# Summing the eight product blocks of each chunk with one strided reduction on VectorE, four transposes of the sums in place of sixteen, and the gate's projection ahead of them

## The chip, the cores and the metric

The kernel runs on one core of one Trainium2 chip. A core has a matrix engine (PE, TensorE), a vector engine (DVE, VectorE), an activation engine (ACT, ScalarE), a general engine (POOL, GpSimd) and a queue engine (SP, SyncE) that here only issues transfers. Each engine works through its own list of instructions in order; semaphores tie the lists together. The metric is device time in microseconds (us), from the median of several runs. Lower is better.

## The reference, cut to what matters

All values are 32-bit floats. `x` and the context are (16, 256, 512): 16 positions, 256 rows, 512 channels-in-time. The 256 rows make 32 heads of 8 rows. The layer is two blocks, each added to its input through a tanh gate:

```python
# block 1, per head h: eight rows i, eight rows j, a causal convolution over l (512)
kv  = einsum('bhil,bhjl->bijhl', ctx, ctx)
y   = causal_conv(kv, ssm_kernel[h]) + kv * D[h]
o[b, j, h, l] = sum over i of  y[b, i, j, h, l] * layernorm(x)[b, h, i, l]
x   = x + tanh(g_xattn) * o
# block 2, per row of 16 positions: a gated mixture-of-two linear attention
z   = layernorm(x);  s = silu(z_prev * w0 + z * w1)
q, k, v, g = silu(s @ Wq), s @ Wk, s @ Wv, s @ Wg
out = (silu(g) * layernorm(attention(q, k, v))) @ Wout
x   = x + tanh(g_ffn) * out
```

The sum over `i` is over eight products. It is this sum that the change makes in another way.

## The kernel before

One pass of the main loop handles one head. On chip, a head's 512 time steps are four chunks of 128 (`CH` = 4), the time step within a chunk lies on the 128 partitions, and the free dimension holds the 8 rows times 16 positions (`ROW` = 128 columns). `kv` is symmetric in i and j, so it is computed by rotations: four rotations of 128 columns and half a rotation, 576 columns a chunk.

The loop is software-pipelined and fully unrolled. `run` calls `step` for h = -2 to 32; a step does the tail of head h-1 (attention output, output projection), the back of head h (projections, scores), the front of head h+1 (convolution, products, sums) and the preparation of head h+2 (products of the context, layer norm). Every engine has its own `step`, written out by hand, so the order of work on an engine is the order of the code, with waits on semaphores between. 31 steps (h = 0 to 30) hold a back and a front.

The part around the change, for one head:

- PE runs the convolution of chunk `lc` into a PSUM bank (`conv`, L282).
- DVE multiplies the bank with the normalised `x` (`multiply`, L733, and for the half rotation `multiply_last`, L770). For each chunk this leaves eight blocks of 128 columns in `z_terms[:, lc, :]`, one for each of the eight rotations or mirrored rotations, which are the eight terms of the sum over i.
- DVE adds the last four blocks onto the first four (`add_halves`, L751, instruction at L756): once for chunks 0 and 1 together (1024 columns out), once each for chunks 2 and 3 (512 columns out). Semaphore `sum_done`.
- PE transposes the remaining four blocks of each chunk and lets PSUM add them up: 16 transposes of 128 x 128 into bank 2 (`add_transposed`, L271, instruction at L277). Semaphore `xo_ps`.
- DVE reads bank 2 and makes the new `x` (`x2`, L889), its statistics (L892 to L900); POOL takes the inverse root (L649), ACT the normalised `z` (L614), with which PE begins the next step (transposes at L268).

What stands behind the transposes of the sums on PE in a step: the gate's projection (`project` into bank 5, 12 matmuls, L426), the transposes of the expanded queries and keys (L428 and L431, which wait for `expand` on DVE, L763 to L768, and for `gatedT_low`, L877, the last reader of bank 7), the output projection of the head before (L440, 12 matmuls), and `scores` (L341), 16 matmuls, which waits among others for `x2_ready` since bank 2 is one of the four score banks. DVE then waits for the output projection (`out_sb`, L913) and masks the scores (L760). ACT copies `gatedT_high` (L588), the two last parts of the context products (`kv_round`, L487), the gate (`gate_sb`, L597), `qeT` and `keT` (L603, L606).

Of the kernel before, what the change touches and what calls it, by code (L numbers as in the profile page):

```python
# [7 lines left out]
ALU = mybir.AluOpType  # L8
ACT = mybir.ActivationFunctionType
F32 = mybir.dt.float32  # L10
F32R = mybir.dt.float32r
AX_X = mybir.AxisListType.X

P = 128
# [15 lines left out]
def flamingo_gated_layer(nc, x, ctx_t, g_xattn, g_ffn, ssm_kernel, ssm_D, conv_w, Wq, Wk, Wv, Wg,  # L30
# [35 lines left out]
    with ExitStack() as stack:  # L66
# [8 lines left out]
        def setup_sb(name, *free):  # L75
            return setup.enter_context(nc.sbuf_tensor(name, [P, *free], F32))
# [51 lines left out]

        setup = ExitStack()
        w_all = setup_sb("w_all", CH, PROJ)  # L130
        w_out = setup_sb("w_out", CH, L)
        w_tmp = z_terms[:, :, 0:DV]
        router = setup_sb("router", RH * HDV, RATIO)
        router_d = setup_sb("router_d", RH * HDV)
        taps = setup_sb("taps", P + L)
        taps_p = setup.enter_context(nc.sbuf_tensor("taps_p", [P, 2, P + L], F32R))
        setup.close()

        y_raw = sb("y_raw", CH, P)
        qk_sb = sb("qk_sb", 2 * RH, HDK)  # L140
        rot_a = sb("rot_a", 2 * RH, HDK)
# [10 lines left out]
        out_sb = sb("out_sb", 2, L)  # L152
        yT_p = parts("yT", CH, P)
        gatedT_p = parts("gatedT", CH, P)
# [110 lines left out]
        def _(eng):  # L265
# [4 lines left out]

            def add_transposed(h1):  # L271


                for c in range(CH):
                    eng.wait_ge(sum_done[max(c, 1)], h1 + 1)
                    for i in range(NROT):
                        ins = nc.tensor.matmul(bank[2][:, c * P:(c + 1) * P], z_terms[:, c, i * ROW:(i + 1) * ROW], ident,  # L277
                                               is_transpose=True, start=(c == 0 and i == 0), stop=(i == NROT - 1),
                                               skip_group_check=True)
                ins.then_inc(xo_ps, 1)  # L280
# [45 lines left out]
            def step(t, p, q, tail, back, front, pre):  # L326
# [85 lines left out]
                if tail:  # L412
# [5 lines left out]
                    transpose4(bank[7], lambda c: gated[:, c * P:(c + 1) * P], gatedT_ps)  # L418
                if front:
                    if pre:  # L420
                        eng.wait_ge(qx_ready, h + 3)
                    add_transposed(h + 1)
                if back:
                    if can_wait(h):
                        eng.wait_ge(mask_done[2], h)
                    project(bank[5], yT_p, w_all_p, G0, DV, g_ps, y_low, h + 1)  # L426
                    eng.wait_ge(qke_ready, h + 1)
                    transpose4(bank[3], lambda c: qke[:, 4 * c:4 * c + 4, :], qeT_ps)  # L428
                    if tail:
                        eng.wait_ge(gatedT_ready, h)  # L430
                    transpose4(bank[7], lambda c: qke[:, RH + 4 * c:RH + 4 * c + 4, :], keT_ps)  # L431
# [15 lines left out]
        def _(eng):  # L447
# [41 lines left out]
            def step(t, p, q, tail, back, front, pre):  # L489
# [94 lines left out]
                if tail:  # L584
                    eng.wait_ge(gatedT_ps, h)
                    if can_wait(h - 1):
                        eng.wait_ge(out_ps, h - 1)
                    eng.activation(gatedT_p[0][:, :, :], bank[7][:, :].rearrange("p (c n) -> p c n", c=CH), ACT.Copy  # L588
                                   ).then_inc(gatedT_high, 1)
                if pre:  # L590
                    kv_round(p, 2, h + 2)
                    kv_round(p, 3, h + 2)
                if back:
                    eng.wait_ge(g_ps, h + 1)
                    if can_wait(h):
                        eng.wait_ge(gated_ready, h)
                    eng.activation(gate_sb[:, :], bank[5][:, :], ACT.Silu).then_inc(gate_ready, 1)  # L597
                if back:
                    eng.wait_ge(qeT_ps, h + 1)
                    if can_wait(h):  # L600
                        for r in range(CH):
# [4 lines left out]
                    eng.activation(keT[:, :, :], bank[7][:, :].rearrange("p (c n) -> p c n", c=CH), ACT.Copy  # L606
                                   ).then_inc(keT_sb, 1)
                if front:
                    eng.wait_ge(rstd2_ready, h + 2)
# [78 lines left out]
        def _(eng):  # L688
# [44 lines left out]
            def multiply(p, lc, h1):  # L733
# [3 lines left out]
                if lc == 0:  # L737
                    eng.wait_ge(qx_ready, h1 + 1)
                    if can_wait(h1):
                        eng.wait_ge(xo_ps, h1)  # L740
                q = qx[:, 1 - p, lc, 0:1]
# [8 lines left out]

            def add_halves(chunks, h1):  # L751

                eng.wait_ge(mul_last, h1 + 1)
                eng.wait_ge(mul_done[chunks.stop - 1], h1 + 1)
                half = NROT * ROW
                eng.tensor_tensor(z_terms[:, chunks, 0:half], z_terms[:, chunks, 0:half], z_terms[:, chunks, half:2 * half],  # L756
                                  ALU.add).then_inc(sum_done[chunks.stop - 1], 1)

# [26 lines left out]
            def step(t, p, q, tail, back, front, pre):  # L785
# [64 lines left out]
                if front:  # L850
                    add_halves(slice(0, 2), h + 1)
                if tail:
# [12 lines left out]
                if front:  # L865
                    multiply(p, 3, h + 1)
                    add_halves(slice(2, 3), h + 1)
                    add_halves(slice(3, 4), h + 1)
                if back:
# [4 lines left out]
                if tail:  # L874
# [3 lines left out]
                                      gatedT_p[0][:, :, :].bitcast(F32), ALU.subtract).then_inc(gatedT_ready, 1)  # L878
                if back:
                    eng.wait_ge(rot_ready, h + 1)  # L880
                    if can_wait(h):
                        eng.wait_ge(keT_ps, h)
                        eng.wait_ge(qeT_ps, h)
                    expand()
                if front:
# [84 lines left out]
```

## Time and profile before

| | us |
|---|---|
| median of 3 runs (lowest, highest) | 923.17 (922.25, 925.02) |
| profiled execution, whole | 923.74 |
| profiled execution, span from first to last instruction | 921.9 |
| PE busy | 856.9 (93% of the span) |
| POOL busy | 730.2 (79%) |
| DVE busy | 720.5 (78%) |
| ACT busy | 435.7 (47%) |

Times in the profile are of one execution. An engine's timeline row gives the start, the time until the last of its instructions ended, the engine, the line, the operation and, in brackets, how long the engine sat idle before it and what ended the wait. Neighbouring instructions of an engine overlap by some tens of nanoseconds, so what an instruction costs its engine is read from one start to the next.

### The profile page before, as it was taken

To read this page: it belongs to the slowest core of one execution; us is meant where nothing else is said; L and a number is where in the kernel's file an instruction comes from. 1 tells how busy PE (TensorE), PEld (TensorE's weight loads), DVE (VectorE), ACT (ScalarE), POOL (GpSimd) and SP (SyncE) were. 2 spreads that over 40 slices of the span, in tenths; PEclk is the share of its full clock that TensorE was granted. 3 is DMA by queue.
4 is the path that set the end of the run, shared out by engine and by line. 5 is a ranking of instruction groups with operands and counts; after the bars stand their busy time and mean duration, and the time that the engine had idled before them with its cause. 6 is when DMAs were issued, how large, how long until landed. Compare 5 with 4: busy or idle time off the path is not lost.

```text
span 921.9 us, 17871 instructions
## 1 busy us (share of the span) xinstructions
PE 856.9 (93%) x6528; PEld 724.3 (79%) x6528; DVE 720.5 (78%) x1528; ACT 435.7 (47%) x938; POOL 730.2 (79%) x613
## 2 busy tenths in 40 slices
PE   0578999999999999999999999999999999999973
PEld 0467888888888888888888888888888888888852
DVE  4867787987778889877787897778878877788742
ACT  2454544545545444554544545545445455454330
POOL 6568898788889888888899888888988888887331
PEclk9889999999999999999999999999999999999996
DMA  8211211222221122222211222222112222210000
GB/s 284 60 53 52 59 26 44 64 63 65 64 64 43 25 61 64 64 64 65 62 34 35 61 64 64 65 63 61 26 42 64 64 64 63 64 46 12 2 12 23
DMA packets 25990, 52.44 MB, mean 57 GB/s; under 512 B 2544, under 2 KB 3696, under 8 KB 25904
## 3 DMA queue, kind: packets, MB, share of 16 engines
q1 hardware_dynamic: 22304, 46.59, 18.7%
q10 hardware_dynamic: 3600, 4.72, 1.6%
q8 instruction: 52, 0.85, 0.4%
q14 instruction: 34, 0.28, 0.1%
HBM read 42.75 MB, written 8.55 MB: 56 GB/s over the span
## 4 chain that ended last, share of the span: by engine, by line
PE 86%; DVE 5%; issue 4%; DMA 1%; ACT 1%; POOL 1%; POOLq 0%; ACTq 0%; DVEq 0%
PE bank L319 37%; PE bank L290 23%; PE bank L268 9%; PE bank L277 6%; PE bank L352 4%; PE bank L337 4%; PE bank L303 2%; DMA w_all<-in_L_ffn_Wv 1%; PE bank L306 1%; DVE z_terms L756 1%; DVE w_all L719 0%; PE bank L402 0%; DVE z_terms L743 0%; DVE w_all_low L725 0%; POOLq L66 0%
## 5 line engine op out<-in xcount | busy, mean ns | idle before, releaser
L290 PE MATMUL bank<-kv_pair,toep 128*128 128x512 f32 x960 | 247.9, 405 | 11.4 <-DVE z_terms L747 6.6
L643 POOL TENSOR_TENSOR kv_pair<-kv,kv_pair 128x576 fp32r<-128x576 f32 x128 | 182.3, 1436 | 54.9 <-ACT kv_pair L487 54.9
L290 PEld LDWEIGHTS bank<-kv_pair,toep 128*128 128x128 f32 x960 | 177.2, 192 | 53.1 <-DVE z_terms L747 12.6
L634 POOL TENSOR_TENSOR kv<-kx 128x512 f32<-128x512 f32 x128 | 174.4, 1363 | 6.7 <-DMA const<-shape_consts 6.7
L649 POOL TENSOR_TENSOR o_rstd<-o_ve,minus_half 128x16 f32<-128x16 f32 x32 | 93.1, 2909 | 82.6 <-DVE o_ve L815 82.6
L487 ACT ACTIVATE kv_pair<-kv 128x576 fp32r<-128x576 f32 x128 | 87.9, 688 | 108.2 <-POOL kv L637 108.2
L319 PE MATMUL bank<-w_all_high,yT_high 128*128 128x512 f32 (+2 forms) x512 | 120.2, 356 | 2.8 <-DVE gated L856 2.8
L756 DVE TENSOR_TENSOR z_terms<-z_terms 128x512 f32<-128x512 f32 (+1 forms) x96 | 117.4, 1249 | 0.0
L319 PE MATMUL bank<-w_all_low,yT_high 128*128 128x512 f32 (+2 forms) x512 | 111.8, 340 | 0.0
L319 PE MATMUL bank<-w_all_high,yT_low 128*128 128x512 f32 (+2 forms) x512 | 106.1, 339 | 0.0
L913 DVE TENSOR_TENSOR out_sb<-bank,x 128x512 f32<-128x512 f32 x32 | 22.1, 691 | 105.6 <-PE bank L319 105.6
L760 DVE TENSOR_TENSOR att<-bank,const 128x512 f32<-128x512 f32 x128 | 79.5, 683 | 16.7 <-PE bank L352 16.7
L319 PEld LDWEIGHTS bank<-w_all_low,yT_high 128*128 128x128 f32 x512 | 83.7, 189 | 11.2
L319 PEld LDWEIGHTS bank<-w_all_high,yT_low 128*128 128x128 f32 x512 | 81.2, 188 | 11.5
L743 DVE TENSOR_TENSOR z_terms<-bank,qx 128x512 f32<-128x512 f32 x128 | 85.4, 667 | 4.3 <-PE bank L290 4.3
L319 PEld LDWEIGHTS bank<-w_all_high,yT_high 128*128 128x128 f32 x512 | 78.9, 190 | 8.9 <-DVE gated L856 3.2
L637 POOL TENSOR_TENSOR kv<-kx 128x64 f32<-128x64 f32 x128 | 73.5, 574 | 0.0
L747 DVE TENSOR_TENSOR z_terms<-bank,qx 128x384 f32<-128x384 f32 x128 | 69.9, 546 | 0.0
L667 POOL TENSOR_TENSOR rot_a<-qk_sb,const 128x512 f32<-128x512 f32 x32 | 66.2, 2069 | 2.5 <-ACT qk_sb L557 2.5
L277 PE MATMUL bank<-const,z_terms 128*128 128x128 f32 x512 | 62.5, 274 | 5.4 <-DVE z_terms L756 5.4
L503 ACT ACTIVATE y_raw<-bank,w_conv 128x128 f32<-128x128 f32 x128 | 36.6, 369 | 61.9 <-PE bank L268 61.9
L649 POOL TENSOR_TENSOR rstd<-ve,minus_half 128x1 f32<-128x1 f32 x64 | 41.2, 643 | 28.3 <-DVE ve L900 22.2
(102 smaller groups left out, 1588.7 us busy)
## 6 DMA issues: line engine op xcount, KB each, us to landing
toep<-taps_dram SPq DMA_DIRECT2D x32, 512.0 KB, 7.1
kx<-in_ctx SPq DMA_DIRECT2D x32, 384.0 KB, 7.4
x_in<-in_x SPq DMA_DIRECT2D x32, 256.0 KB
out_x<-out_sb SPq DMA_DIRECT2D x32, 256.0 KB
w_all<-in_L_ffn_Wv ACTq DMA_DIRECT2D x1, 1024.0 KB, 11.9
w_all<-in_L_ffn_Wg ACTq DMA_DIRECT2D x1, 1024.0 KB, 9.9
w_out<-in_L_ffn_Wout ACTq DMA_DIRECT2D x1, 1024.0 KB, 16.2
router<-in_L_ffn_router_w ACTq DMA_DIRECT2D x1, 512.0 KB, 7.3
```

Of the source, the lines that this page charges most:

```text
L268: ins = nc.tensor.transpose(dst[:, c * P:(c + 1) * P], src(c), ident)
L277: ins = nc.tensor.matmul(bank[2][:, c * P:(c + 1) * P], z_terms[:, c, i * ROW:(i + 1) * ROW], ident, is_transpose=True, start=(c == 0 and ...
L290: ins = nc.tensor.matmul(bank[lc % 2][:, :], toep[:, 1 - p, a, (lc - mc) * P:(lc - mc + 1) * P], kv_p[b][:, 1 - p, mc, 0:FULL], start=(mc ...
L319: ins = nc.tensor.matmul(dst[:, 0:cols], src_p[a][:, c, :], w_p[b][:, c, c0:c0 + cols], start=(i == 0 and c == 0), stop=(i == len(PASSES) ...
L487: eng.activation(kv_p[0][:, p, c, :], kv[:, c % 2, :], ACT.Copy).then_inc(kv_high[c], 1)
L634: eng.tensor_tensor(view(kv[:, c % 2, 0:FULL], [[ROW, NROT], [1, ROW]]), view(kx[:, p, c, 0:ROW], [[0, NROT], [1, ROW]]), view(kx[:, p, c, ...
L637: eng.tensor_tensor(kv[:, c % 2, FULL:FULL + HALF], kx[:, p, c, 0:HALF], kx[:, p, c, HALF:2 * HALF], ALU.mult).then_inc(kv_made[c], 1)
L643: eng.tensor_tensor(kv_p[1][:, p, c, :], kv[:, c % 2, :], kv_p[0][:, p, c, :].bitcast(F32), ALU.subtract).then_inc(kv_ready[c], 1)
L649: eng.tensor_tensor(dst[:, 0:n], src[:, 0:n], minus_half[:, 0:n], ALU.pow).then_inc(done, 1)
L743: eng.tensor_tensor(view(z_terms[:, lc, 0:1], [[ROW, NROT], [1, ROW]]), view(y[:, 0:1], [[ROW, NROT], [1, ROW]]), view(q, [[NB, NROT], [1, ...
L756: eng.tensor_tensor(z_terms[:, chunks, 0:half], z_terms[:, chunks, 0:half], z_terms[:, chunks, half:2 * half], ALU.add).then_inc(sum_done[ ...
L760: eng.tensor_tensor(att[:, r, :, :], bank[SCORE_BANKS[r]][:, :].rearrange("p (c n) -> p c n", c=CH), view(mask[:, 0:1], [[0, CH], [1, P]]) ...
```

## The change

- `add_halves` goes. In its place `sum_terms` issues one `tensor_reduce` a chunk, four a head: 128 outputs, each the sum of eight inputs. The view puts the rotation innermost with a step of `ROW` = 128 floats (512 bytes), so each instruction reads 1024 floats of `z_terms`, and no two that follow each other are neighbours in memory. The result goes into `z_sum`, which is the buffer `y_raw` under another name.
- `add_transposed` with its 16 transposes becomes `transpose_sums` with 4, on `z_sum`.
- On PE the gate's projection moves ahead of the transposes of the sums.
- On ACT the gate's copy moves ahead of `kv_round` 2, and `kv_round` 3 moves behind the copy of `keT`.
- On DVE `expand` moves ahead of `ratio` and `gatedT_low`.
- The wait on `xo_ps` moves from `multiply` of chunk 0 (which now waits on the last `sum_done` of the head before) into `sum_terms`. Two setup buffers and `yT` change their place in SBUF.

```diff
-            def add_transposed(h1):
+            def transpose_sums(h1):
                 for c in range(CH):
-                    eng.wait_ge(sum_done[max(c, 1)], h1 + 1)
-                    for i in range(NROT):
-                        ins = nc.tensor.matmul(bank[2][:, c * P:(c + 1) * P], z_terms[:, c, i * ROW:(i + 1) * ROW], ident,
-                                               is_transpose=True, start=(c == 0 and i == 0), stop=(i == NROT - 1),
-                                               skip_group_check=True)
+                    eng.wait_ge(sum_done[c], h1 + 1)
+                    ins = nc.tensor.transpose(bank[2][:, c * P:(c + 1) * P], z_sum[:, c, :], ident)
                 ins.then_inc(xo_ps, 1)
...
+                if back:
+                    if can_wait(h):
+                        eng.wait_ge(mask_done[2], h)
+                    project(bank[5], yT_p, w_all_p, G0, DV, g_ps, y_low, h + 1)
                 if front:
                     if pre:
                         eng.wait_ge(qx_ready, h + 3)
-                    add_transposed(h + 1)
-                if back:
-                    if can_wait(h):
-                        eng.wait_ge(mask_done[2], h)
-                    project(bank[5], yT_p, w_all_p, G0, DV, g_ps, y_low, h + 1)
+                    transpose_sums(h + 1)
...
-            def add_halves(chunks, h1):
+            def sum_terms(c, h1):
                 eng.wait_ge(mul_last, h1 + 1)
-                eng.wait_ge(mul_done[chunks.stop - 1], h1 + 1)
-                half = NROT * ROW
-                eng.tensor_tensor(z_terms[:, chunks, 0:half], z_terms[:, chunks, 0:half], z_terms[:, chunks, half:2 * half],
-                                  ALU.add).then_inc(sum_done[chunks.stop - 1], 1)
+                eng.wait_ge(mul_done[c], h1 + 1)
+                if can_wait(h1):
+                    eng.wait_ge(xo_ps, h1)
+                eng.tensor_reduce(z_sum[:, c, :], view(z_terms[:, c, 0:1], [[1, ROW], [ROW, 2 * NROT]]), AX_X, ALU.add
+                                  ).then_inc(sum_done[c], 1)
...
-                    add_halves(slice(0, 2), h + 1)
+                    sum_terms(0, h + 1)
+                    sum_terms(1, h + 1)
...
-                    add_halves(slice(2, 3), h + 1)
-                    add_halves(slice(3, 4), h + 1)
+                    sum_terms(2, h + 1)
+                    sum_terms(3, h + 1)
+                if back:
+                    eng.wait_ge(rot_ready, h + 1)
+                    if can_wait(h):
+                        eng.wait_ge(keT_ps, h)
+                        eng.wait_ge(qeT_ps, h)
+                    expand()
```

PE, from the transposes of `gated` to the output projection, in the kernel before (`qke` holds expanded queries and keys, bank 5 is the gate's):

```order
L268 MATMUL bank7<-const,gated 128x128 x4
L277 MATMUL bank2<-const,z_terms 128x128 x16
L319 MATMUL bank5<-w_all_high,yT_high 128x512 x4
L319 MATMUL bank5<-w_all_low,yT_high 128x512 x4
L319 MATMUL bank5<-w_all_high,yT_low 128x512 x4
L268 MATMUL bank3<-const,qke 128x128 x4
```

The same stretch of PE in the changed kernel, where `y_raw` is the buffer that holds the sums:

```order
L269 MATMUL bank7<-const,gated 128x128 x4
L317 MATMUL bank5<-w_all_high,yT_high 128x512 x4
L317 MATMUL bank5<-w_all_low,yT_high 128x512 x4
L317 MATMUL bank5<-w_all_high,yT_low 128x512 x4
L277 MATMUL bank2<-const,y_raw 128x128 x4
L269 MATMUL bank3<-const,qke 128x128 x4
```

The 12 matmuls of the gate stand ahead of the sums, and the transposes of the sums are 4; the transposes of `qke` follow them directly.

DVE, from the selection masks to the new `x`, in the kernel before:

```order
L842 TENSOR_SCALAR u<-bank6 128x16
L756 TENSOR_TENSOR z_terms<-z_terms 128x2x512
L856 TENSOR_TENSOR gated<-bank4,o_rstd 128x512
L861 TENSOR_TENSOR gated<-gated,gate_sb 128x512
L864 RECIPROCAL rth1<-th1 128x16
L743 TENSOR_TENSOR z_terms<-bank1,qx 128x512
L747 TENSOR_TENSOR z_terms<-bank1,qx 128x3x128
L756 TENSOR_TENSOR z_terms<-z_terms 128x512 x2
L873 TENSOR_TENSOR ratio<-rth1,bank6 128x16
L877 TENSOR_TENSOR gatedT_low<-bank7,gatedT_high 128x512
L765 TENSOR_TENSOR qke<-rot_a,sel 128x1024
L889 SCALAR_TENSOR_TENSOR x2<-bank2,gates,x_in 128x512
```

The same stretch of DVE in the changed kernel:

```order
L843 TENSOR_SCALAR u<-bank6 128x16
L757 TENSOR_REDUCE y_raw<-z_terms 128x128 x2
L858 TENSOR_TENSOR gated<-bank4,o_rstd 128x512
L863 TENSOR_TENSOR gated<-gated,gate_sb 128x512
L866 RECIPROCAL rth1<-th1 128x16
L743 TENSOR_TENSOR z_terms<-bank1,qx 128x512
L747 TENSOR_TENSOR z_terms<-bank1,qx 128x3x128
L757 TENSOR_REDUCE y_raw<-z_terms 128x128 x2
L766 TENSOR_TENSOR qke<-rot_a,sel 128x1024
L881 TENSOR_TENSOR ratio<-rth1,bank6 128x16
L885 TENSOR_TENSOR gatedT_low<-bank7,gatedT_high 128x512
L891 SCALAR_TENSOR_TENSOR x2<-bank2,gates,x_in 128x512
```

Two reductions stand where one add of two chunks stood, ahead of the `gated` pair; two where two adds of one chunk stood; and `expand` (`qke`) is ahead of `ratio` and `gatedT_low`.

## Rows read from the trace of the kernel before

**Rows 1.** The page, part 1: busy time and share of the span.

```profile
PE 856.9 (93%) x6528; PEld 724.3 (79%) x6528; DVE 720.5 (78%) x1528; ACT 435.7 (47%) x938; POOL 730.2 (79%) x613
```

**Rows 2.** The page, part 4: the chain that ended last, by engine.

```profile
PE 86%; DVE 5%; issue 4%; DMA 1%; ACT 1%; POOL 1%; POOLq 0%; ACTq 0%; DVEq 0%
```

**Rows 3.** The view of waits: who waited for whom, total us, times, longest.

```profile
DVE out_sb L913 <- PE bank L319: 105.6, 32, 4.4
...
DVE yT_low L807 <- ACT y_raw L528: 25.9, 32, 2.3
```

**Rows 4.** The chain in order of time, one step: start, us, what.

```profile
416.21 0.44 PE bank L268 x4
416.65 1.75 PE bank L277 x16
418.40 2.78 PE bank L319 x12
...
422.05 2.75 PE bank L319 x12
```

**Rows 5.** Timeline of PE, same step: start, length, operation.

```profile
421.02 1.03 PE L268 MATMUL bank<-const,qke 128*128 128x128 f32 x8
...
424.73 1.17 PE L352 MATMUL bank<-qeT,keT 32*128 32x128 f32 x32
```

**Rows 6.** Timeline of DVE, the same step.

```profile
399.47 2.48 DVE L760 TENSOR_TENSOR att<-bank,const 128x512 f32<-128x512 f32 x4 [0.39 <-PE bank L352]
...
411.05 1.22 DVE L756 TENSOR_TENSOR z_terms<-z_terms 128x1024 f32<-128x1024 f32 x1
412.18 0.69 DVE L856 TENSOR_TENSOR gated<-bank,o_rstd 128x512 f32<-128x512 f32 x1
...
415.06 2.43 DVE L756 TENSOR_TENSOR z_terms<-z_terms 128x512 f32<-128x512 f32 x2
417.41 0.16 DVE L873 TENSOR_TENSOR ratio<-rth,bank 128x16 f32<-128x16 f32 x1
...
418.09 1.56 DVE L765 TENSOR_TENSOR qke<-rot_a,sel 128x1024 f32<-128x1024 f32 x1
419.58 0.74 DVE L889 SCALAR_TENSOR_TENSOR x<-bank,gates,x_in 128x512 f32<-128x512 f32 x1
...
424.84 0.69 DVE L913 TENSOR_TENSOR out_sb<-bank,x 128x512 f32<-128x512 f32 x1 [3.25 <-PE bank L319]
425.93 2.48 DVE L760 TENSOR_TENSOR att<-bank,const 128x512 f32<-128x512 f32 x4 [0.39 <-PE bank L352]
```

**Rows 7.** Groups by form on DVE: count, busy us, mean ns, idle before.

```profile
L756 DVE TENSOR_TENSOR z_terms<-z_terms 128x512 f32<-128x512 f32 x64 | 76.0, 1226 | 0.0
...
L812 DVE TENSOR_REDUCE o_var<-o_sq 128x16 f32<-128x512 f32 x32 | 22.0, 687 | 7.3 <-ACT o_sq L533 4.4
...
L702 DVE TENSOR_TENSOR router_d<-router 128x512 f32<-128x512 f32 x1 | 1.7, 1700 | 0.7 <-DMA w_all<-in_L_ffn_Wv 0.7
```

**Rows 8.** Single lines, L756 and L765: shortest, median, longest duration in ns.

```profile
L756 DVE TENSOR_TENSOR z_terms<-z_terms x96: 673/1216/2219, 41.7 to 866.2; 128x512 f32<-128x512 f32 x64, 128x1024 f32<-128x1024 f32 x32
...
L765 DVE TENSOR_TENSOR qke<-rot_a,sel x32: 1215/1559/1842, 73.3 to 891.9; 128x1024 f32<-128x1024 f32 x32
```

**Rows 9.** Timeline of POOL: beside L702 at 14.67 us, and beside step 399.47.

```profile
14.61 1.21 POOL L634 TENSOR_TENSOR kv<-kx 128x512 f32<-128x512 f32 x1
15.78 0.77 POOL L637 TENSOR_TENSOR kv<-kx 128x64 f32<-128x64 f32 x1
...
421.59 0.55 POOL L649 TENSOR_TENSOR rstd<-ve,minus_half 128x1 f32<-128x1 f32 x1 [0.28 <-DVE ve L900]
```

**Rows 10.** Timeline of ACT, the same step.

```profile
423.76 0.81 ACT L614 ACTIVATE z<-x,nmr,rstd 128x512 f32<-128x512 f32 x1
```

**Rows 11.** Timeline of DVE, step h = -1.

```profile
41.72 1.34 DVE L756 TENSOR_TENSOR z_terms<-z_terms 128x1024 f32<-128x1024 f32 x1
...
46.08 0.75 DVE L889 SCALAR_TENSOR_TENSOR x<-bank,gates,x_in 128x512 f32<-128x512 f32 x1 [0.75 <-PE bank L277]
```

More of the change, by code:

```diff
@@ L129, in flamingo_gated_layer @@
         setup = ExitStack()
+        taps = setup_sb("taps", P + L)
+        taps_p = setup.enter_context(nc.sbuf_tensor("taps_p", [P, 2, P + L], F32R))
         w_all = setup_sb("w_all", CH, PROJ)
@@ L134, in flamingo_gated_layer @@
         router_d = setup_sb("router_d", RH * HDV)
-        taps = setup_sb("taps", P + L)
-        taps_p = setup.enter_context(nc.sbuf_tensor("taps_p", [P, 2, P + L], F32R))
         setup.close()
         y_raw = sb("y_raw", CH, P)
+        z_sum = y_raw
+        yT_p = parts("yT", CH, P)
         qk_sb = sb("qk_sb", 2 * RH, HDK)
@@ L152, in flamingo_gated_layer @@
         out_sb = sb("out_sb", 2, L)
-        yT_p = parts("yT", CH, P)
         gatedT_p = parts("gatedT", CH, P)
@@ L418, in step @@
                     transpose4(bank[7], lambda c: gated[:, c * P:(c + 1) * P], gatedT_ps)
-                if front:
-                    if pre:
-                        eng.wait_ge(qx_ready, h + 3)
-                    add_transposed(h + 1)
                 if back:
@@ L426, in step @@
                     project(bank[5], yT_p, w_all_p, G0, DV, g_ps, y_low, h + 1)
+                if front:
+                    if pre:
+                        eng.wait_ge(qx_ready, h + 3)
+                    transpose_sums(h + 1)
+                if back:
                     eng.wait_ge(qke_ready, h + 1)
@@ L589, in step @@
                                    ).then_inc(gatedT_high, 1)
-                if pre:
-                    kv_round(p, 2, h + 2)
-                    kv_round(p, 3, h + 2)
                 if back:
@@ L597, in step @@
                     eng.activation(gate_sb[:, :], bank[5][:, :], ACT.Silu).then_inc(gate_ready, 1)
+                if pre:
+                    kv_round(p, 2, h + 2)
                 if back:
@@ L607, in step @@
                                    ).then_inc(keT_sb, 1)
+                if pre:
+                    kv_round(p, 3, h + 2)
                 if front:
@@ L739, in multiply @@
                     if can_wait(h1):
-                        eng.wait_ge(xo_ps, h1)
+                        eng.wait_ge(sum_done[CH - 1], h1)
                 q = qx[:, 1 - p, lc, 0:1]
@@ L878, in step @@
                                       gatedT_p[0][:, :, :].bitcast(F32), ALU.subtract).then_inc(gatedT_ready, 1)
-                if back:
-                    eng.wait_ge(rot_ready, h + 1)
-                    if can_wait(h):
-                        eng.wait_ge(keT_ps, h)
-                        eng.wait_ge(qeT_ps, h)
-                    expand()
                 if front:
```

## The prediction

> **What bounds the kernel now.** I read the busy shares first: PE is at 93%, DVE at 78%, POOL at 79% [rows 1]. Then the chain that ended last: 86% of it is PE [rows 2]. So PE sets the pace, and the waits agree: the largest wait of DVE is for PE's output projection, 105.6 us in 32 times, 3.3 us a step [rows 3]. That wait is the slack that DVE has in a step. Last I read one step as a timeline of DVE and as the chain of PE. Masks begin at 399.47 and again at 425.93, so a step takes 26.46 us [rows 6], and there are 31 such steps. I count time in a step from 399.47, so that the masks stand at t = 0.
>
> **The change on PE.** The 16 transposes of the sums take 1.75 us of the chain, 0.109 each; four others take 0.44 [rows 4]. Twelve go, so PE saves 1.31 us a step and its own work falls to 26.46 - 1.31 = 25.15 us. If nothing else were late, that would be 31 x 1.31 = 41 us, or 883 us. The gate's projection is 2.78 us [rows 4], the same before and after; standing first, it gives the sums that much more time.
>
> **The change on DVE.** Before, the sums cost DVE 412.18 - 411.05 = 1.13 us for chunks 0 and 1, and 417.41 - 415.06 = 2.35 us for chunks 2 and 3, in all 3.48 us a step [rows 6]. The second pair is dear because POOL reads at the same time: an add of 512 columns takes 1.226 us on average [rows 7], but the shortest of the line takes 0.673 [rows 8].
>
> After, there are four reductions of 1024 inputs. Nothing in the trace reads single floats 512 bytes apart, so I bound one reduction, R, from both sides. The low end: a reduction of 512 neighbouring inputs takes 0.687 us [rows 7], and the add of 1024 columns takes 1.22 [rows 6], 0.55 more than the shortest add of 512; with that slope R = 0.69 + 0.53 = 1.22 us. No row on DVE goes below this rate for 32-bit data, so I exclude a lower one. The high end: one instruction reads single floats, every second one, for both of its operands: L702, 512 columns in 1.700 us [rows 7]. Taken whole, less 0.16 us of fixed cost (0.69 less 0.53), that is 3.0 ns a column and R = 3.24 us.
>
> L702 is the row nearest in kind, but POOL worked beside it, and POOL's second instruction there took 0.77 us [rows 9], so part of the 1.700 is contention. An add of the same size under contention takes 1.226 on average [rows 7]. I put the rest, 0.474 us or 0.93 ns a column, down to the step. It was paid with two stepped operands, the reduction has one. Between half of it (0.46) and all of it (0.93) I take the middle, 0.69 ns a column, so R = 1.22 + 1024 x 0.69 ns = 1.93 us. The ends are kept for the range. What speaks against this: the first POOL instruction beside L702 ended at 15.82, and L702 ended at 16.37, which is 0.55 us later, as long as 512 columns take at the full rate. If DVE merely stood behind POOL, stepping by 8 bytes cost nothing. It remains that 512 bytes is another step than 8.
>
> The Trainium skill has a measured rule on this ("Vector Engine (DVE) Microarchitecture Reference", section Measured stream behaviour on trn2): a port keeps its full rate only while consecutive elements come as at least two neighbouring words, and a source that hops at every element cost 1.73 ns a column where a contiguous one cost 1.05. By that page R would be about 1.92 us, an estimate. It also names an exception, a one-source operation hopping between two regions and writing one word per two reads, which ran at the full rate; by that R would be 1.22. No row here shows either.
>
> **What a step takes after.** An instruction of 1.22 us costs DVE 1.13, as the next one starts 0.09 earlier [rows 6]; so a reduction costs s = R - 0.09. Along DVE and then PE:
>
> - from the masks to the first sum, unchanged: 411.05 - 399.47 = 11.58;
> - two sums: 2s; then the `gated` pair, the reciprocal and the products of chunk 3, unchanged: 415.06 - 412.18 = 2.88; two sums: 2s;
> - `expand`: 418.09 to 419.58 is 1.49 beside POOL, but its shortest is 1.215 [rows 8], so 1.15 if POOL has finished its products by then, which it has when DVE is late; `ratio` and `gatedT_low`: 418.09 - 417.41 = 0.68;
> - about 0.1 for the semaphore, then PE: the second four transposes of `qke`, which write bank 7 after `gatedT_low` has read it, 0.44; the output projection 2.75 [rows 4]; and from its end at 424.80 to the next masks at 425.93, 1.13, in which PE runs the scores [rows 5]. (The transposes of `qke` themselves are the eight of 421.02 [rows 5].)
>
> That is 11.58 + 2.88 + 1.15 + 0.68 + 0.1 + 0.44 + 2.75 + 1.13 + 4s = 20.71 + 4s. With R = 1.93, s = 1.84 and the step is 28.07 us, 1.61 more than before. PE, with 25.15 us of work, waits about 2.9 us a step: some 0.3 for `gated` (it moves back by 2s - 1.13 = 2.55 us, and had about 2.2 of room), some 1.5 in front of the sums, the rest for `expand` and `gatedT_low`. What hides behind what: the new `x` starts at t = 23.65 instead of 20.11. From it to the end of `z` is 5.0 us before [rows 6, 10], but 1.2 of that is ACT still busy when POOL's root was ready at 422.14 [rows 9]; the true chain is about 3.8, so `z` is there at 27.5, before PE wants it at about 28.0. The `scores` wait for `x` is met too, as 24.4 is before 27. ACT's moves cost nothing: ACT is busy 47% [rows 1], and the copies that PE waits for come first. POOL's last parts of the context products wait behind the root and land some 2 us later against the step; POOL's work of 730.2 us is 23 us a step and fits in 28.
>
> In step h = -1 PE is idle and the sums lie on the chain: from 41.72 to the new `x` at 46.08 [rows 11]. Four sums for three adds: 4 x 1.84 - 2.54 = +4.8, and the last transposes take some 0.4 less: +4.4 us.
>
> The sum: 923.7 + 31 x 1.61 + 4.4 = 978 us. The profiled execution (923.74, its span 921.9) is 0.6 above the median of 923.17, so this is 978 for the median too.
>
> **The rivals.**
>
> 1. *The strided read runs at the full rate: faster.* R = 1.22, s = 1.13. The chain gives 20.71 + 4.52 = 25.23, and with `expand` still beside POOL 25.57, against PE's 25.15. So 0.89 to 1.3 us a step are won: 923.7 - 31 x 0.89 + 1.6 = 898, at best 885. For it: 0.55 us after POOL in L702 [rows 7, 9], the reduction of one source at the full rate, and that it stands out of POOL's way. Against it: the inputs have no neighbours at all. The two cases part at 4s = 26.46 - 20.71, so R = 1.53 us: below it the kernel is faster, above it slower. This is also the result of the skill's exception.
> 2. *The step costs what both operands of L702 paid, or more.* R = 2.17 gives s = 2.08 and a step of 29.03: 923.7 + 31 x 2.57 + 5.4 = 1009 us. At R = 3.24 the step is 33.3 and the time about 1146. For it: L702 as it stands. Against it: the contention in it.
> 3. *R lands beside the break-even of 1.53* and the loss and the gain cancel: 920 to 926. No row speaks for that rate.
>
> **How the numbers follow.** Forecast (R from 1.6 to 2.15, 933 to 1007 us, likeliest 978): 0.46. Rival 1: 0.38. Rival 2 beyond 1007: 0.14. Rival 3: 0.02. Since cases of both signs hold most of the chance, the forecast's own range is 950 to 1005. The range for 8 in 10 goes from 886, which takes in most of rival 1, to 1012, which leaves out most of rival 2. A difference under 0.3% (3 us) could not be told from none. Faster 0.38; same 0.02; slower 0.60.
>
> **What would show it.** In the changed profile, first the mean duration of the reduction L757: 1.9 us in my case, 1.2 in rival 1, over 2.1 in rival 2. Then the distance between two rows of masks: 28.1, or 25.2 to 25.6. PE in front of the transposes of `y_raw` (L277) should wait for L757 about 1.5 us a step, and DVE's wait for the output projection should shrink from 3.3 to about 1.4. POOL's products beside the second pair of sums should lose their long instances. I am wrong if L757 is at 1.2, or if DVE has a shorter way to the output projection than the sum above, which a step well under 20.71 + 4s would show.

## The result and the profile after

The changed kernel takes 1006.27 us (median of 4 runs, 1006.01 to 1006.53) against 923.63 us for the kernel before in the same session. The ratio is 1.0895 with a 95% interval of 1.0876 to 1.0914: it is slower by 9%. The forecast was 978 us, slower, for the reason that the strided reduction is dear on DVE. The direction and the reason held; the size was 55 us forecast against 83 measured. The time lies near the upper end of the range for 8 in 10 (886 to 1012) and 1 us above the narrower one, 950 to 1005.

The page of the changed kernel: busy shares, and two of its costliest groups (count, busy us, mean ns, idle before and its releaser).

```profile
PE 862.4 (86%) x6144; PEld 708.6 (71%) x6144; DVE 848.8 (85%) x1560; ACT 442.4 (44%) x938; POOL 645.2 (64%) x613
...
L757 DVE TENSOR_REDUCE y_raw<-z_terms 128x128 f32<-128x1024 f32 x128 | 245.6, 1959 | 0.0
...
L317 PE MATMUL bank<-w_all_high,yT_high 128*128 128x512 f32 (+2 forms) x512 | 129.9, 378 | 64.5 <-DVE gated L858 64.5
```

Against [rows 1], DVE gained 128 us of work and PE, with 384 matmuls fewer, is no less busy, 862.4 us: part of its matmuls ran slower, as shown below (the granted clock was 0.941 over the span, against 0.976 in the kernel before). One reduction takes 1.96 us; I had estimated 1.93.

The waits of the changed kernel, who waited for whom, total us, times, longest:

```profile
PE bank L317 <- DVE gated L858: 64.5, 31, 2.4
DVE out_sb L915 <- PE bank L317: 56.6, 32, 4.8
...
PE bank L277 <- DVE y_raw L757: 11.3, 6, 2.9
PE bank L269 <- DVE qke L766: 9.5, 12, 0.8
```

DVE's slack in front of the output projection fell from 105.6 [rows 3] to 56.6 us. PE now waits 2.1 us a step, but not where I had put it: in front of the `v` projection, for `gated`, and hardly in front of the sums. The 0.8 us for `qke` come in 12 of the steps only.

One step on DVE in the changed kernel, from masks to masks, to be laid beside [rows 6]:

```profile
436.69 2.48 DVE L761 TENSOR_TENSOR att<-bank,const 128x512 f32<-128x512 f32 x4 [0.39 <-PE bank L350]
...
448.24 3.84 DVE L757 TENSOR_REDUCE y_raw<-z_terms 128x128 f32<-128x1024 f32 x2
452.00 0.68 DVE L858 TENSOR_TENSOR gated<-bank,o_rstd 128x512 f32<-128x512 f32 x1
452.71 1.44 DVE L863 TENSOR_TENSOR gated<-gated,gate_sb 128x512 f32<-128x512 f32 x1
...
455.24 3.89 DVE L757 TENSOR_REDUCE y_raw<-z_terms 128x128 f32<-128x1024 f32 x2
459.05 1.21 DVE L766 TENSOR_TENSOR qke<-rot_a,sel 128x1024 f32<-128x1024 f32 x1
...
460.26 0.68 DVE L885 TENSOR_TENSOR gatedT_low<-bank,gatedT_high 128x512 fp32r<-128x512 f32 x1
460.86 0.74 DVE L891 SCALAR_TENSOR_TENSOR x<-bank,gates,x_in 128x512 f32<-128x512 f32 x1
...
464.45 0.69 DVE L915 TENSOR_TENSOR out_sb<-bank,x 128x512 f32<-128x512 f32 x1 [1.57 <-PE bank L317]
465.53 2.48 DVE L761 TENSOR_TENSOR att<-bank,const 128x512 f32<-128x512 f32 x4 [0.39 <-PE bank L350]
```

The step is 28.84 us instead of 26.46. The four sums take 3.76 + 3.81 = 7.57 us from start to start, before 3.48. Up to 448.24 nothing has moved (11.55 us, before 11.58). From 460.86, where `gatedT_low` has ended, to the next masks it is 4.67 us. The second instruction of the `gated` pair, L863, takes 1.44 us where L861 took 1.06 (both medians of 32). It reads two tiles in SBUF, and POOL multiplies beside it:

```profile
452.38 1.22 POOL L634 TENSOR_TENSOR kv<-kx 128x512 f32<-128x512 f32 x1
```

And on PE, the part of the same step where it waits:

```profile
449.99 0.63 PE L269 MATMUL bank<-const,qn 128*128 128x128 f32 x4
452.73 1.19 PE L317 MATMUL bank<-w_all_high,yT_high 128*128 128x512 f32 x4 [2.11 <-DVE gated L858]
...
458.83 0.68 PE L277 MATMUL bank<-const,y_raw 128*128 128x128 f32 x4
460.31 1.34 PE L269 MATMUL bank<-const,qke 128*128 128x128 f32 x8 [0.80 <-DVE qke L766]
461.41 1.16 PE L317 MATMUL bank<-w_out_high,gatedT_high 128*128 128x512 f32 x4
```

In 18 of the 30 steps PE lost clock, in nearly all of them from the `v` projection on, behind that wait. One of them, with the busy time of one of its stretches (length, then PE, PEld, DVE, ACT, POOL with counts, the granted clock, DMA share, GB/s):

```profile
510.43 2.07 PE L317 MATMUL bank<-w_all_high,yT_high 128*128 128x512 f32 x4 [2.12 <-DVE gated L858]
...
518.54 1.04 PE L269 MATMUL bank<-const,qke 128*128 128x128 f32 x8
```

```profile
510.50:513.80 3.30, 3.30 (x8) 2.62 (x9) 3.30 (x5) 0.00 (x0) 2.97 (x4) 0.50 0.00 0
```

Four matmuls take 2.07 us there instead of 1.19. PE comes to the transposes of `qke` so much later that it no longer waits for them, and so the step is only 0.24 us longer, 29.09 instead of 28.85.

Where the 82.1 us between the two spans (1004.0 and 921.9) lie: the masks that end step h = 0 come at 86.43 instead of 81.10, +5.3; the 30 steps from there on take 29.02 us on average instead of 26.50, +75.5; the end takes +1.2.

### The profile page after: what moved, and what is told of

Same layout as the page of the kernel before. It is cut to its first block and busy times, and to the rows that moved or that the text cites. A ratio compares the mean times of both kernels' runs of the same rounds, so it can differ in the third digit from the quotient of the medians.

```text
span 1004.0 us, 17167 instructions
## 1 busy us (share of the span) xinstructions
PE 862.4 (86%) x6144; PEld 708.6 (71%) x6144; DVE 848.8 (85%) x1560; ACT 442.4 (44%) x938; POOL 645.2 (64%) x613
## 5 line engine op out<-in xcount | busy, mean ns | idle before, releaser
L757 DVE TENSOR_REDUCE y_raw<-z_terms 128x128 f32<-128x1024 f32 x128 | 245.6, 1959 | 0.0
L317 PE MATMUL bank<-w_all_high,yT_high 128*128 128x512 f32 (+2 forms) x512 | 129.9, 378 | 64.5 <-DVE gated L858 64.5
L634 POOL TENSOR_TENSOR kv<-kx 128x512 f32<-128x512 f32 x128 | 159.8, 1248 | 6.6 <-DMA const<-shape_consts 6.6
L317 PE MATMUL bank<-w_all_low,yT_high 128*128 128x512 f32 (+2 forms) x512 | 123.4, 366 | 0.0
L317 PE MATMUL bank<-w_all_high,yT_low 128*128 128x512 f32 (+2 forms) x512 | 112.2, 353 | 0.0
L317 PEld LDWEIGHTS bank<-w_all_low,yT_high 128*128 128x128 f32 x512 | 91.4, 204 | 13.7
L317 PEld LDWEIGHTS bank<-w_all_high,yT_low 128*128 128x128 f32 x512 | 87.0, 199 | 13.8
L582 ACT ACTIVATE v_sb<-bank 128x512 f32<-128x512 f32 x32 | 19.2, 598 | 163.5 <-PE bank L317 163.5
L915 DVE TENSOR_TENSOR out_sb<-bank,x 128x512 f32<-128x512 f32 x32 | 22.1, 692 | 56.6 <-PE bank L317 56.6
L637 POOL TENSOR_TENSOR kv<-kx 128x64 f32<-128x64 f32 x128 | 55.4, 433 | 0.0
L593 ACT ACTIVATE gate_sb<-bank 128x512 f32<-128x512 f32 x32 | 19.1, 598 | 68.6 <-PE bank L317 68.6
```

Source lines behind the costliest of these rows:

```text
L317: ins = nc.tensor.matmul(dst[:, 0:cols], src_p[a][:, c, :], w_p[b][:, c, c0:c0 + cols], start=(i == 0 and c == 0), stop=(i == len(PASSES) ...
L634: eng.tensor_tensor(view(kv[:, c % 2, 0:FULL], [[ROW, NROT], [1, ROW]]), view(kx[:, p, c, 0:ROW], [[0, NROT], [1, ROW]]), view(kx[:, p, c, ...
L637: eng.tensor_tensor(kv[:, c % 2, FULL:FULL + HALF], kx[:, p, c, 0:HALF], kx[:, p, c, HALF:2 * HALF], ALU.mult).then_inc(kv_made[c], 1)
L757: eng.tensor_reduce(z_sum[:, c, :], view(z_terms[:, c, 0:1], [[1, ROW], [ROW, 2 * NROT]]), AX_X, ALU.add).then_inc(sum_done[c], 1)
```

## The experiments

**What a step between floats costs on DVE, by itself.** A kernel of its own, which computes nothing of the layer. Its core, each line four times:

```diff
+ tensor_reduce, 1024 floats in, 128 out: [[8, 128], [1, 8]]; [[16, 128], [2, 8]]; [[32, 128], [4, 8]]; [[1, 128], [24, 8]]; [[1, 128], [128, 8]]; [[1, 128], [1024, 8]]
+ tensor_reduce over two axes, pairs of neighbours: [[2, 128], [256, 4], [1, 2]]
+ add of 512 columns: contiguous; both operands at step 2; one, then both at step 128; writing at step 2, then at step 64
+ beside POOL multiplying: the contiguous add; the reduction at step 128
```

> A kernel of its own that computes nothing of the layer: groups of four DVE instructions on fixed data, each group with another step between the floats read or written, POOL idle; in the last two groups POOL multiplies beside. Theory (a step over more than a pair of neighbours slows a DVE stream, about 0.7 ns a column, whatever the other load): the reduction of 1024 inputs takes 1.22 us contiguous, 1.22 at a step of 2 floats, near 1.9 to 2.7 at steps of 4 and 24, 1.95 at 128 and 1024, and 1.22 again when it reads pairs of neighbours that lie 256 floats apart. The add of 512 columns takes 0.69 contiguous and 0.69 with both operands at step 2 (so that the 1.70 us of L702 was POOL's doing), 1.05 with one operand or both at step 128, 0.69 writing at step 2, 1.05 writing at step 64. Rival (it is the reduction itself that is slow with 128 results of 8): 1.95 at every step. Beside POOL: the contiguous add 1.2, the stepped reduction 1.96 as without POOL.

Timeline of DVE, one instruction of most groups in that order (start, length):

```profile
31.99 1.21 DVE L56 TENSOR_REDUCE dst<-src 128x128 f32<-128x1024 f32 x1
...
36.63 1.21 DVE L56 TENSOR_REDUCE dst<-src 128x128 f32<-128x1024 f32 x1
...
41.98 1.94 DVE L56 TENSOR_REDUCE dst<-src 128x128 f32<-128x1024 f32 x1
...
50.20 2.61 DVE L56 TENSOR_REDUCE dst<-src 128x128 f32<-128x1024 f32 x1
...
59.68 1.86 DVE L56 TENSOR_REDUCE dst<-src 128x128 f32<-128x1024 f32 x1
...
73.51 1.21 DVE L90 TENSOR_REDUCE dst<-src 128x128 f32<-128x1024 f32 x1
...
79.54 0.69 DVE L60 TENSOR_TENSOR dst<-src,two 128x512 f32<-128x512 f32 x1
...
84.89 1.02 DVE L60 TENSOR_TENSOR dst<-src,two 128x512 f32<-128x512 f32 x1
...
87.09 1.25 DVE L60 TENSOR_TENSOR dst<-src,two 128x512 f32<-128x512 f32 x1
...
92.48 0.69 DVE L60 TENSOR_TENSOR dst<-src,two 128x512 f32<-128x512 f32 x1
...
100.94 1.74 DVE L60 TENSOR_TENSOR dst<-src,two 128x512 f32<-128x512 f32 x1
...
109.76 1.87 DVE L56 TENSOR_REDUCE dst<-src 128x128 f32<-128x1024 f32 x1
```

The reduction takes 1.21 us contiguous and at step 2, 1.94 at step 4, 2.61 at step 24, 1.86 at steps 128 and 1024, and 1.21 again by pairs 256 floats apart (L90). The adds: 0.69 at step 2 for both operands (79.54 lies in that group), 1.02 with one operand at step 128, 1.22 to 1.25 with both, 0.69 writing at step 2, 1.03 writing at step 64. So it is the step that costs, 0.63 ns a column at 128, and not the reduction; the rival falls. The cost begins between 2 and 4 floats: at step 2 no two floats that are read are neighbours, and yet nothing is paid. My 1.05 for both operands was too low. Beside POOL the contiguous add takes 1.74, where I had expected 1.2, and the stepped reduction 1.85 to 1.91, nearly as without POOL. The two results for the add account for L702: at step 2 alone it would take 0.69, and beside POOL even a contiguous one takes as long as its 1.700 [rows 7]. The two together were not run.

**The changed kernel with contiguous reads.** It sums the wrong terms.

```diff
-                eng.tensor_reduce(z_sum[:, c, :], view(z_terms[:, c, 0:1], [[1, ROW], [ROW, 2 * NROT]]), AX_X, ALU.add
+                eng.tensor_reduce(z_sum[:, c, :], view(z_terms[:, c, 0:1], [[2 * NROT, ROW], [1, 2 * NROT]]), AX_X, ALU.add
```

> The changed kernel with one difference: each reduction reads 1024 neighbouring floats (8 in a row for each result) instead of floats 512 bytes apart. It leaves out the right sum: wrong terms are added. Theory (the step is the whole cost): R falls from 1.96 to 1.22, DVE's chain from 28.84 to about 25.8 to 26.1 us a step, so 905 to 915 us, ratio to the kernel before 0.98 to 0.99. Rival 1 (the reduction costs 1.96 whatever it reads): 1006. Rival 2 (the wait of the v projection for gated, which forecast overlooked, holds the step even then): gated still stands behind two sums, 2.26 in place of 1.13, and since PE had only about 0.3 us there, some 0.8 us of the 1.31 saved on PE are lost: step 25.9; the two agree on the time, and the idle time of PE in front of the v projection tells it: 0.6 to 0.9 us a step.

915.25 us, ratio to the kernel before 0.9885 (0.9870 to 0.9899). The group, and PE in front of the `v` projection:

```profile
L757 DVE TENSOR_REDUCE y_raw<-z_terms 128x128 f32<-128x1024 f32 x128 | 149.3, 1206 | 0.0
```

```profile
434.81 1.19 PE L317 MATMUL bank<-w_all_high,yT_high 128*128 128x512 f32 x4 [0.68 <-DVE gated L858]
```

```profile
434.78 1.80 DVE L863 TENSOR_TENSOR gated<-gated,gate_sb 128x512 f32<-128x512 f32 x1
```

Four reductions of 0.75 us less, and an L863 that is dearer again, make a step of 26.14 (mean over 30 steps 26.17). The step between the floats is worth 91 us of the 1006, all of the loss and more. But without it the change still wins only 10 us and not the 25 to 38 that my first rival gave it. L863, which here meets other instructions of POOL, takes 1.70 us from start to start (1.36 in the changed kernel, 0.98 before), and that lies on DVE's chain, which sets the step. PE's path is hardly shorter: idle 0.68 us for `gated`, it then runs without a pause up to the transposes of `qke`, of which the last four wait some 0.15 us for `gatedT_low` (the eight take 0.94 us to the next start, 0.79 in the kernel before). So with a cheap L863 the wait for `gated` would still have held the step at about 26.0, an estimate (26.14 less 0.15): the two limits stand side by side.

**The pair `gated` ahead of the first two sums.** The waiting place that I had overlooked, taken away in the changed kernel.

```diff
-                if front:
-                    sum_terms(0, h + 1)
-                    sum_terms(1, h + 1)
                 if tail:
...
+                if front:
+                    sum_terms(0, h + 1)
+                    sum_terms(1, h + 1)
                 if back:
                     eng.wait_ge(th1_ready, h + 1)
```

> The changed kernel with the first two reductions moved behind the gated pair on DVE. Theory (DVE's own chain up to the second pair of sums sets the step, and PE's 2.1 us of idle time in front of the v projection is only slack shown in another place): PE's idle time moves to the transposes of the sums, step 28.5 to 28.9, 996 to 1007 us. Rival (the v projection's wait for gated sets the step, through v, gated and gate projections, 6 us of PE behind it): about 2 us a step less, 940 to 950 us.

1031.53 us, ratio 1.1145 (1.1129 to 1.1162): slower than the changed kernel by 25 us, which neither theory had said. Timeline of PE, from the gate's projection on:

```profile
468.40 0.33 PE L277 MATMUL bank<-const,y_raw 128*128 128x128 f32 x1 [0.38 <-DVE y_raw L757]
470.20 0.33 PE L277 MATMUL bank<-const,y_raw 128*128 128x128 f32 x1 [1.48 <-DVE y_raw L757]
471.34 1.46 PE L269 MATMUL bank<-const,qke 128*128 128x128 f32 x8 [0.81 <-DVE qke L766]
472.44 2.05 PE L317 MATMUL bank<-w_out_high,gatedT_high 128*128 128x512 f32 x4
474.30 1.79 PE L317 MATMUL bank<-w_out_low,gatedT_high 128*128 128x512 f32 x4
475.93 1.09 PE L317 MATMUL bank<-w_out_high,gatedT_low 128*128 128x512 f32 x4
```

Busy time by stretch, in the same columns as above. The first row is another step, whole, in which the clock stayed up:

```profile
389.01:417.68 28.67, 25.89 (x193) 21.11 (x194) 25.60 (x48) 13.43 (x29) 18.42 (x19) 1.00 0.19 51
...
472.44:474.30 1.86, 1.86 (x8) 1.47 (x6) 1.35 (x7) 1.35 (x3) 0.40 (x1) 0.50 0.00 0
474.30:475.93 1.63, 1.63 (x6) 1.30 (x4) 0.00 (x0) 1.11 (x2) 1.63 (x3) 0.53 0.00 0
475.93:476.95 1.02, 1.02 (x5) 0.56 (x3) 0.00 (x0) 0.00 (x0) 1.02 (x1) 1.00 0.00 0
```

The move did shift PE's idle time to the sums, as the theory had it, and the steps in which the clock stayed up take 28.68 us, the length of DVE's chain. But PE now stood idle three times close together, 2.7 us in all, and then the granted clock was at 0.50, the 1.2 GHz level, for some 3.4 us, just when the output projection ran: 4.51 us instead of 2.93. Such steps take 30.1 to 30.3 us, and the mean is 29.93. The changed kernel loses clock nearly as often, in 18 of 30 steps against 22 here, but it pays 0.24 us for it and this order 1.5: there a wait of PE stands behind the slow matmuls and takes them in, here the output projection runs slowly while DVE waits for it. What lets some steps keep their clock behind the same three waits, as the one at 389.01, is not known.

**The same with useless work where PE waits.** Six matmuls that nobody reads, ahead of the last transpose of the sums:

```diff
                 for c in range(CH):
+                    if c == CH - 1 and filler:
+                        for k in range(6):
+                            nc.tensor.matmul(bank[3][:, :], yT_p[0][:, k % CH, :], w_all_p[0][:, k % CH, G0:G0 + DV],
+                                             start=True, stop=True)
                     eng.wait_ge(sum_done[c], h1 + 1)
...
```

> The changed kernel with the gated pair ahead of the first reductions (the experiment that took 1031 us), and on PE six matmuls of 512 columns in front of the last transpose of the sums, whose result is never read: some 1.4 us of useless work a step, placed where PE waits for DVE. Theory (in that experiment DVE's chain is 28.7 us, and the steps of 30.2 us come from PE's clock, which was at half for some 3.4 us after waits of 0.4, 1.5 and 0.8 us close together): with the wait filled the clock stays up, every step takes 28.7 to 28.9 us, 992 to 1002 us, the faster for more work. Rival (the length of the step comes from something else in that order, as the ACT or POOL order): 1030 or more.

998.74 us, ratio 1.0808 (1.0789 to 1.0826). The masks of two steps that follow each other:

```profile
460.31 2.48 DVE L765 TENSOR_TENSOR att<-bank,const 128x512 f32<-128x512 f32 x4 [0.39 <-PE bank L354]
...
489.08 2.48 DVE L765 TENSOR_TENSOR att<-bank,const 128x512 f32<-128x512 f32 x4 [0.39 <-PE bank L354]
```

Steps of 28.77 us, 28.78 on average, none of them at 30.2: 33 us less for more work. The rival falls, and this is shown for the clock: 1031 was DVE's chain plus the half clock that followed PE's idle time. It also says what the overlooked wait was worth in the changed kernel: with the wait gone and the clock up, the step is 28.77 against 28.84, so next to nothing.

**The order alone.** The kernel before with its 16 transposes and its adds, and the change's moves on PE, ACT and DVE:

```diff
-                    add_transposed(h + 1)
-                if back:
                     if can_wait(h):
                         eng.wait_ge(mask_done[2], h)
                     project(bank[5], yT_p, w_all_p, G0, DV, g_ps, y_low, h + 1)
+                if front:
+                    if pre:
+                        eng.wait_ge(qx_ready, h + 3)
+                    add_transposed(h + 1)
...
```

> The kernel before with the change's order alone: gate projection ahead of the 16 transposes, gate copy first and the last kv part after keT on ACT, expand ahead of ratio and gatedT_low on DVE; the adds of halves stay. Theory (PE is busy all the time and the order costs nothing): 921 to 927 us, same as before. Rival (the new x comes 1.7 us later, and so does z, with which PE begins the next step): up to 0.3 us a step, 930 to 934 us.

923.72 us, ratio 0.9982 (0.9969 to 0.9996): within 0.3%, so the order costs nothing where PE's work sets the step. In the changed kernel, where DVE's chain does, it was not tried by itself.

**The sums by pairs.** Terms k and k + 4 of a column lie side by side, so that the reduction reads neighbours; the whole sum is computed. The products of the half rotation are written in the same layout.

```diff
-                eng.tensor_tensor(view(z_terms[:, lc, 0:1], [[ROW, NROT], [1, ROW]]),
+                eng.tensor_tensor(view(z_terms[:, lc, 0:1], [[2 * ROW, NROT], [2, ROW]]),
...
-                first = 4 * ROW + NB
-                eng.tensor_tensor(view(z_terms[:, lc, first:first + 1], [[ROW + NB, NROT - 1], [1, ROW]]),
+                first = 2 * NB + 1
+                eng.tensor_tensor(view(z_terms[:, lc, first:first + 1], [[2 * (ROW + NB), NROT - 1], [2, ROW]]),
...
-                eng.tensor_reduce(z_sum[:, c, :], view(z_terms[:, c, 0:1], [[1, ROW], [ROW, 2 * NROT]]), AX_X, ALU.add
+                eng.tensor_reduce(z_sum[:, c, :], view(z_terms[:, c, 0:1], [[2, ROW], [2 * ROW, NROT], [1, 2]]), mybir.AxisListType.XY, ALU.add
...
```

> The changed kernel with another layout of the products: terms k and k+4 of a column lie side by side (even and odd floats), so the products are written at a step of 2 floats and each reduction reads pairs of neighbours. It computes the whole sum. Theory (a stream is slowed only when it has no neighbour to read or write with; the group of reductions by pairs took 1.21 us and the add that writes at step 2 took 0.69, as contiguous): reductions 1.21, products as before, step 26.1 us as with contiguous reads, 911 to 918 us. Rival (the writes at step 2 cost as hops do, in the products read from PSUM, 1152 columns a chunk at 0.6 ns, 2.8 us a step): 990 to 1005.

916.25 us, ratio 0.9913 (0.9897 to 0.9930). Groups by form:

```profile
L757 DVE TENSOR_REDUCE y_raw<-z_terms 128x128 f32<-128x1024 f32 x128 | 149.3, 1205 | 0.0
L743 DVE TENSOR_TENSOR z_terms<-bank,qx 128x512 f32<-128x512 f32 x128 | 85.3, 667 | 4.5 <-PE bank L288 4.5
```

The reductions take 1.205 us, and the products, which now write at step 2, still 667 ns. It is the change made good: 90 us less than the changed kernel by the layout alone, and within 1 us of the kernel with contiguous reads.

**Pairs, and the pair `gated` first.** The two edits together.

> The paired layout and the gated pair ahead of the first two reductions on DVE. Theory (with contiguous reads PE still stood idle 0.68 us a step in front of the v projection, since two reductions stand ahead of gated; without that wait DVE's chain of about 20.9 + 4 x 1.13 sets the step): 25.4 to 25.8 us, 893 to 905 us. Rival (POOL's reads slow the moved instructions as much as is won): 26.1, 911 to 918 us.

899.38 us, ratio 0.9729 (0.9711 to 0.9747), the fastest of all kernels run, 2.7% below the kernel before. The step is 25.67 on average. Its parts, from DVE's timeline:

```profile
426.01 1.30 DVE L860 TENSOR_TENSOR gated<-gated,gate_sb 128x512 f32<-128x512 f32 x1
...
434.12 0.68 DVE L885 TENSOR_TENSOR gatedT_low<-bank,gatedT_high 128x512 fp32r<-128x512 f32 x1
434.72 0.74 DVE L891 SCALAR_TENSOR_TENSOR x<-bank,gates,x_in 128x512 f32<-128x512 f32 x1
...
439.39 2.48 DVE L761 TENSOR_TENSOR att<-bank,const 128x512 f32<-128x512 f32 x4 [0.39 <-PE bank L350]
```

From the end of `gatedT_low` (434.72) to the masks it is 4.67 us, to the hundredth as in the changed kernel. So DVE's chain still sets the step, 0.5 us above PE's 25.15. What shortened it by 0.48 us is one instruction: the second of the pair (L860 here, L863 before the move) takes 1.23 from start to start instead of 1.71, beside other instructions of POOL. That the place against POOL makes this price is read from the timelines; no run moved POOL's work alone. PE's wait for `gated` is gone as well, and without that the step could not have fallen below about 26.0. The same move cost 25 us with reductions of 1.96 us, through the clock, and saves 17 with reductions of 1.21, where the clock fell in none of the 30 steps.

**And `expand` ahead of the last two sums**, with the transposes of the queries ahead of those of the sums on PE.

> As the one before, and expand ahead of the last two reductions on DVE, the transposes of the expanded queries ahead of those of the sums on PE. Theory (PE's work of 25.15 us a step is then the bound): 25.2 to 25.5 us, 884 to 896 us. Rival (expand then runs beside POOL's products and the new x, 3.8 us ahead of z, is what PE waits for): no better than the kernel before it, 893 to 905 us.

910.60 us, ratio 0.9861 (0.9841 to 0.9880): slower than the one before it by 11 us. I missed this one. DVE's timeline:

```profile
437.28 1.58 DVE L767 TENSOR_TENSOR qke<-rot_a,sel 128x1024 f32<-128x1024 f32 x1
```

`expand` reads two SBUF operands, and here it meets POOL: 1.58 us instead of 1.21. Its place gives nothing back, because `gatedT_low` stands at the end of the same chain of DVE wherever `expand` is. The steps take 26.03 us, 0.37 more than 25.66, which is that 0.37.

## Why the prediction came out as it did

- *R = 1.93 us*: measured 1.96. The value was right, and half of its argument was wrong. I put 0.474 us of L702 down to a step of 2 floats; alone that step costs nothing (0.69), and POOL alone makes 1.74 of a contiguous add. The sign that I wrote down against myself, that L702 ended 0.55 us after POOL's first instruction, fits this. The extra at 512 bytes is real, but no row of the trace before had it: I took a middle between half and all of a figure that was POOL's doing, and that it came within 0.03 us is luck. The estimate from the Trainium skill's measured table ("Vector Engine (DVE) Microarchitecture Reference", section Measured stream behaviour on trn2), 1.92, was the sounder ground, and the trace is near it, 1.86 alone and 1.96 in the kernel. Its exception for one-source operations did not apply to eight regions. Its condition for the full rate, neighbouring words, is too strict for what was measured: the step of 2 floats ran at the full rate without any.
- *The step of 20.71 + 4s, 28.07 us*: 28.84 while the clock was up, 0.77 more. The form held, as the kernels with R = 1.21 and R = 1.96 show, but three terms were small: the four sums take 7.57, not 7.36 (+0.21); the stretch from the `gated` pair to the last sums takes 3.24, not 2.88, since L863 takes 1.44 where it took 1.06 (+0.36); and from `gatedT_low` to the masks it is 4.67, not 4.42 (+0.25). The other terms give 0.05 back. The last of the three is an error of reading. From the start of the output projection to the masks it is 4.12 in both kernels (421.81 to 425.93, 461.41 to 465.53), of which I counted 2.75 + 1.13: the chain view begins the projection only where the transposes before it have ended, at 422.05 [rows 4].
- *The whole, in the span*: 82.1 measured, 54.3 forecast (31 x 1.61 + 4.4), 27.8 missed. In the 30 steps from masks to masks the terms above make 23 and the steps above 28.84 another 5, less 1 since the kernel before has long steps too (26.50 on average). Up to the first masks it is 0.7 less than forecast (5.3 for 4.4 + 1.6), and the end takes 1.2 more.
- *The clock*: not in the sum. In 18 of 30 steps PE ran some matmuls at half clock after its wait. The mean step of 29.02 against 28.84 makes it at most 0.18 us a step, 5 us. The experiment with 1031 us has the effect where nothing takes it in.
- *Where PE waits*: wrong. I put 0.3 us in front of the transposes of `gated` and 1.5 in front of the sums. It is 2.1 in front of the `v` projection, which waits for `gated` to have read bank 4 (`o_normed`, L410), one place earlier in PE's order than the place I looked at. For the time of the forecast it did not matter, since DVE's chain was the longer; with cheap reductions it comes within 0.15 us of that chain.
- *Rival 1, 898 us at the full rate*: the mechanism has been tried and gives 915. Against the rival's sum of 25.23, DVE's chain is longer by 0.71 us from the `gated` pair to the last sums, through L863, and by the same 0.25 from `gatedT_low` to the masks. The sum had taken both from the kernel before as unchanged. PE's wait for `gated`, also not foreseen, would have held the step at about 26.0 by itself, by the estimate above.
- *Step h = -1, +4.4*: right. The new `x` of that step comes at 50.49 instead of 46.08 [rows 11], +4.41. The first masks belong to the step after it, which lost only 0.9 us more.
- *ACT, POOL, the new x and z cost nothing*: right for ACT, `x` and `z`: up to the first sum the step is as before (11.55), and from `gatedT_low` on only PE's own work is left. POOL did cost something, the 0.36 us by which it slows L863. Without the reductions the order alone makes no difference.

## What to carry to other kernels

Sum blocks of 32-bit floats on DVE only with a layout in which the next float read lies close: steps of 1 and 2 floats and pairs of neighbours ran at the full rate, a step of 4 already did not. Interleaving two terms at write time was free and took a reduction from 1.96 to 1.21 us. When work moves from the full engine to one with slack, follow every result that stands behind the moved work on the receiving engine, not only the moved work's own reader; here the second reader, the `v` projection, would have kept all but 0.45 us a step of the 1.31 that PE had saved. An instruction on the receiving engine that reads two tiles in SBUF may also change its price when it moves against POOL: L863 took from 1.06 to 1.79 us in these kernels. And a wait on PE can cost more than its length: before moving one, see what PE runs right behind it.

## What the runs showed of the hardware that was not expected

- An experiment that only moved two instructions made the kernel 25 us slower, and six useless matmuls a step took 33 us off again; the granted clock was 0.50 behind three waits of 0.38, 1.48 and 0.81 us, and 1.00 behind the one wait of 2.11 us in the step shown of the changed kernel. Other steps of that kernel did lose clock behind the same wait, and some steps of the experiment did not behind the same three; what tells these steps apart was not settled.
- A step of 24 floats (2.61 us a reduction) costs more than steps of 4 (1.94), 128 or 1024 (1.86).
- A reduction at step 128 takes 1.86 us alone, 1.85 to 1.91 beside POOL and 1.96 in the kernel. What adds the 0.1 was not tried.
- A contiguous add beside a POOL that never pauses takes 1.74 us, against the 1.226 that the kernel's adds had on average [rows 7]. POOL's own multiply goes from 1.26 to 1.70 beside it, and back to 1.26 beside the stepped reduction.
